# Attention and mixture-of-experts layer on one core: FFN steps spread over other slots, VectorE's exponential in two halves, loop branches announced

## What is computed

```python
def wl_step(acc, wl):
    cpm, iw = wl
    ...
    scores = jnp.einsum('bhqd,bhkd->bhqk', Qw, Kw) * SCALE
    scores = scores * jnp.cos(KERR * scores * scores)
    attn = jax.nn.softmax(scores, axis=-1)
    out = jnp.einsum('bhqk,bhkd->bhqd', attn, V)
    return (acc + out * iw, None)
...
logits = x @ router_w + router_b
probs = jax.nn.softmax(logits, axis=-1)
top_v, top_i = jax.lax.top_k(probs, TOP_K)
...
h = jax.nn.gelu(jnp.einsum('btd,edf->ebtf', x, w1), approximate=False)
y = jnp.einsum('ebtf,efd->ebtd', h, w2)
out = jnp.einsum('bte,ebtd->btd', gates[..., :E], y) + gates[..., E:] * x
...
x = _layernorm(x + _L0_attn_ref(x, ...), axis=-1)
x = _layernorm(x + _L0_ffn_ref(x, ...), axis=-1)
```

## Time and profile before

| | |
|---|---|
| median of 3 runs | 7504.47 us (7492.89 to 7508.42) |
| the profiled execution's own time | 7501.78 us |
| its span | 7500.2 us, 125933 instructions |
| ACT busy | 6970.5 us (93%) |
| PE busy | 6103.0 us (81%) |
| DVE busy | 5752.1 us (77%) |
| granted clock, mean | 0.93 |
| ACT line 556 (the exponentials) | 2048 instructions, 6765.2 us busy, mean 3392 ns, 318.5 us idle before them |
| PE line 626 (the weighings) | 30720 matmuls, 4092.8 us busy, mean 644 ns |

### The profile page before, as it was taken

How to read it: one execution, slowest core, us unless ns; L and a number is a source line. 1 busy time by engine, 2 the same in 40 slices (tenths; PEclk the granted TensorE clock), 3 DMA queues, 4 the chain that set the end, 5 groups by cost and what they waited for, 6 DMA issues and landing times.

```text
span 7500.2 us, 125933 instructions
## 1 busy us (share of the span) xinstructions
PE 6103.0 (81%) x46020; PEld 2156.8 (29%) x46020; DVE 5752.1 (77%) x7952; ACT 6970.5 (93%) x2227; POOL 117.5 (2%) x243
## 2 busy tenths in 40 slices
PE   6888887787888878888888888888888887888877
PEld 2222222222223322323232223222232332332325
DVE  4777777777787787778777787878787777877873
ACT  4999999999999999999999999999999999999992
POOL 0000000000000000000000000000000000000000
PEclk7999999999999999999999999999999999999998
DMA  2000000000000000001000000000010000000000
GB/s 57 4 4 4 2 4 4 4 5 13 28 15 26 28 15 28 22 20 31 22 24 28 14 27 25 18 28 19 25 31 17 26 28 14 28 22 21 28 18 35
DMA packets 61179, 152.18 MB, mean 20 GB/s; under 512 B 10272, under 2 KB 28576, under 8 KB 60320
## 3 DMA queue, kind: packets, MB, share of 16 engines
q1 hardware_dynamic: 59808, 142.14, 6.7%
q0 software_dynamic: 768, 1.57, 0.1%
HBM read 132.66 MB, written 11.01 MB: 19 GB/s over the span
## 4 chain that ended last, share of the span: by engine, by line
ACT 38%; PE 21%; issue 21%; DVE 14%; ACTq 5%; DMA 0%; DVEq 0%; SPq 0%
ACT ring L556 37%; PE pv L626 13%; ACTq L551 3%; DVE scores L762 3%; DVE vprobs L780 2%; DVE vprobs L781 2%; PE pv L633 2%; PE sc L609 1%; PE sc L598 1%; PE tr L642 1%; DVE vbits L779 1%; DVE vpower L777 1%; DVE ring L778 1%; DVE vbits L776 1%; PE sc L1076 1%
## 5 line engine op out<-in xcount | busy, mean ns | idle before, releaser
L556 ACT ACTIVATE ring<-scores 128x4096 f32<-128x4096 f32 (+3 forms) x2048 | 6765.2, 3392 | 318.5 <-PE pv L626 262.7
L626 PE MATMUL pv<-ring,vh 128*32 128x512 f32 x30720 | 4092.8, 644 | 1099.0 <-ACT ring L556 1053.7
L626 PEld LDWEIGHTS pv<-ring,vh 128*32 128x32 f32 x30720 | 1018.9, 116 | 3826.8 <-issue 2297.7
L788 DVE COPY numer<-pv 128x512 f32<-128x512 f32 x512 | 353.1, 690 | 913.5 <-PE pv L633 906.3
L752 DVE TENSOR_REDUCE rowmax<-sc 128x1 f32<-128x1024 f32 x512 | 602.1, 1217 | 163.4 <-PE sc L590 163.4
L781 DVE SCALAR_TENSOR_TENSOR vprobs<-vprobs,vbits 128x1024 f32<-128x1024 f32 x512 | 627.2, 1225 | 17.6
L780 DVE SCALAR_TENSOR_TENSOR vprobs<-ring 128x1024 f32<-128x1024 f32 x512 | 627.3, 1225 | 17.5
L782 DVE SCALAR_TENSOR_TENSOR vprobs<-ring,vprobs 128x1024 f32<-128x1024 f32 x512 | 627.2, 1225 | 17.6
L762 DVE COPY scores<-sc 128x1024 f32<-128x1024 f32 (+1 forms) x512 | 601.7, 1216 | 31.3 <-PE sc L609 30.7
L633 PE MATMUL pv<-vprobs,vlast 128*32 128x512 f32 x2048 | 530.4, 593 | 12.3 <-DVE vprobs L782 10.3
L633 PE MATMUL pv<-vpower,vlast 128*32 128x512 f32 x2048 | 529.6, 592 | 0.0
(11 more groups left out here) (159 smaller groups left out, 2684.0 us busy)
## 6 DMA issues: line engine op xcount, KB each, us to landing
tile_w<-in_L_ffn_w SPq DMA_DIRECT2D x192, 512.0 KB, 3.9
qt<-q_scratch SPq DMA_DIRECT2D x256, 36.0 KB
kt_<-k_scratch SPq DMA_DIRECT2D x256, 36.0 KB
ring<-in_L_ffn_w SPq DMA_DIRECT2D x2, 2048.0 KB, 12.3
scores<-in_L_attn_x SPq DMA_DIRECT2D x4, 512.0 KB, 4.8
q_scratch<-qt SPq DMA_DIRECT2D x4, 512.0 KB, 3.8
k_scratch<-kt_ SPq DMA_DIRECT2D x4, 512.0 KB, 4.0
v_scratch<-vv SPq DMA_DIRECT2D x4, 512.0 KB, 3.4
```

The costliest lines, as they stand in the source:

```text
L556: nc.scalar.activation(ring[:, i % SLOTS, 0:cols], scores[:, bass.ds(n % 2, 1), half * CK:(half + 1) * CK, :].rearrange("p o k s -> p (o k ...
L626: last = nc.tensor.matmul(sums, vh[:, buf, half * CK + k, :], ring[:, 2 * half + w2, col:col + HALF], start=(half == 0 and k == 0), stop=( ...
```

## The change

- **FFN steps.** In the first head TensorE's four single steps lie at steps 5, 9, 11 and 13 (before 5, 6, 7 and ahead of 8), VectorE's pieces at steps 5, 10, 11 and 13 (`TILE_SLOTS`). The slices go from steps 11 to 14 to steps 12 to 15. In the second head the parts of the second matmul go from 11 to 14 to 10 to 13, the gates from step 6 to step 4, and `tile_finish` is split: four additions at step 12 (`add_experts`, as soon as two parts are there), four at 13, then the layer norm at 13.
- **Guards.** TensorE's transposes of the numerators wait for the tile copies that share their PSUM tile at quarters 2 and 3, and those at the end for the logits; the projection and the router wait for `tr_read`.
- **ScalarE** takes the logits' exponential directly ahead of the Gelu, behind the first quarter of the second head.
- **Exponential in halves.** `exponents` (four operations) runs at even steps, `polynomials` (three) at odd ones; before, all seven ran at odd steps. The last step of a head was that of the next head's first set; now steps 14 and 15 are.

```diff
@@ scalar_main
-                quads(n, 0, 3)
+                quads(n, 0, 4)
+                quads(n + 1, 0, 1)
                 act.wait_ge(tile_logits_made, i + 1)
                 nc.scalar.activation(t_ex, t_lg, ACT.Exp).then_inc(tile_exp, 1)
-                quads(n, 3, 4)
-                quads(n + 1, 0, 1)
                 act.wait_ge(tile_hidden_copied, 4 * (i + 1))
...
@@ head_products
-                    if quad == 2 and wi == 0 and part == 1 and tile_no is not None:
-                        tile_router(pe, tile_no)
...
-                        if quad == 2 and part == 1 and tile_no is not None:
-                            pe.wait_ge(tile_logits_made, tile_no + 1)
+                        if part == 1 and tile_no is not None and quad == 2:
+                            pe.wait_ge(tile_attT_made, tile_no + 1)
+                        if part == 1 and tile_no is not None and quad == 3:
+                            pe.wait_ge(tile_x1T_made, tile_no + 1)
                         transpose_numer(pe, n, quad - 1)
...
-                        if quad == 1 and wi:
-                            if wi == 1:
-                                tile_attention(pe, tile_no, n)
-                            elif wi == 2:
-                                tile_projection(pe, tile_no)
-                            else:
-                                tile_transpose(pe, tile_no)
-                        elif 11 <= at < 15:
-                            tile_slice(pe, tile_no, n + 1, at - 11)
-                    if tile_no is not None and part == 2 and 11 <= at < 15:
-                        tile_part_two(pe, tile_no, n + 1 if more else n, at - 11)
+                        if at == 5:
+                            tile_attention(pe, tile_no, n)
+                        elif at == 9:
+                            tile_projection(pe, tile_no, n)
+                        elif at == 11:
+                            tile_transpose(pe, tile_no)
+                        elif at == 13:
+                            tile_router(pe, tile_no, n)
+                        if at >= 12:
+                            tile_slice(pe, tile_no, n + 1, at - 12)
+                    if tile_no is not None and part == 2 and 10 <= at < 14:
+                        tile_part_two(pe, tile_no, n + 1 if more else n, at - 10)
+            if part == 1 and tile_no is not None:
+                pe.wait_ge(tile_logits_made, tile_no + 1)
             transpose_numer(pe, n, 3)
...
-            with pe.Fori(0, PAIRS - FIRST_PAIR - 1) as i:
+            with nc.Fori(0, PAIRS - FIRST_PAIR - 1, engines=TENSOR_ONLY, hint_back_edge=True) as i:
...
@@ exponentials becomes exponents (to the fourth operation) and
+        def polynomials(dve, m, pair):
+            base = VSTEPS * (8 * m + pair)
+            probs = vprobs[:, pair % 2, :]
+            dve.wait_ge(vexp_step, base + 4)
...
+        def add_experts(dve, i, half, then):
+
+            dve.wait_ge(tile_parts, 4 * i + 2 * half + 2 + START)
+            for e in range(half * NE // 2, (half + 1) * NE // 2):
...
@@ vector_head
-                    if at == 8 and part == 1:
-                        tile_part_one_vector(dve, i, 3, then)
...
-                    if quad == 1 and wi and part == 1:
-                        tile_part_one_vector(dve, i, wi - 1, then)
-                    if 11 <= at < 15 and part == 1:
-                        copy_hidden(dve, i, at - 11)
-                    if at == 14 and part == 2:
+                    if at in TILE_SLOTS and part == 1:
+                        tile_part_one_vector(dve, i, TILE_SLOTS.index(at), then)
+                    if at >= 12 and part == 1:
+                        copy_hidden(dve, i, at - 12)
+                    if at in (12, 13) and part == 2:
+                        add_experts(dve, i, at - 12, then)
+                    pair = at // 2 + 1
+                    if pair < 8:
+                        (exponents if at % 2 == 0 else polynomials)(dve, n, pair)
+                    elif more:
+                        (exponents if at % 2 == 0 else polynomials)(dve, n + 1, 0)
+                    if at == 4 and part == 2:
+                        tile_gates(dve, i, then)
+                    if at == 13 and part == 2:
                         tile_finish(dve, i, then)
-                    if at == 6 and part == 2:
-                        tile_gates(dve, i, then)
-                    if at % 2 == 1 and at < 15:
-                        exponentials(dve, n, at // 2 + 1)
-                    elif at == 15 and more:
-                        exponentials(dve, n + 1, 0)
...
+        TILE_SLOTS = (5, 10, 11, 13)
```

More of the change, by code:

```diff
@@ L739, in tensor_main @@
                 shifted_tile(pe, 0, k)
-            with pe.Fori(0, FIRST_PAIR) as i:
+            with nc.Fori(0, FIRST_PAIR, engines=TENSOR_ONLY, hint_back_edge=True) as i:
                 head_products(pe, 2 * i, part=1)
                 head_products(pe, 2 * i + 1, part=2)
-            with pe.Fori(0, PAIRS - FIRST_PAIR - 1) as i:
+            with nc.Fori(0, PAIRS - FIRST_PAIR - 1, engines=TENSOR_ONLY, hint_back_edge=True) as i:
                 n = 2 * (i + FIRST_PAIR)
@@ L762, in copy_scores, with exponents @@
             nc.vector.tensor_copy(scores[:, bass.ds(m % 2, 1), k, :].rearrange("p o s -> p (o s)"), sc[:, use % 2, :]).then_inc(sc_free, 1)
-        def exponentials(dve, m, pair, first=False):
+        def exponents(dve, m, pair, first=False):
             base = VSTEPS * (8 * m + pair)
             score = scores[:, bass.ds(m % 2, 1), KT - 1, :].rearrange("p o s -> p (o s)")
-            bits, mant, power, probs = vbits[:, :], vmant, vpower[:, pair % 2, :], vprobs[:, pair % 2, :]
+            bits, power = vbits[:, :], vpower[:, pair % 2, :]
             then = stepper(dve, vexp_step, base, [0])
@@ L838, in tile_gates @@
             then(nc.vector.scalar_tensor_tensor(tile_z[:, :], tile_x1[:, :], t_route[6][:, 0, NE:NE + 1], tile_x1[:, :], ALU.mult, ALU.add))
-        def tile_finish(dve, i, then):
-            dve.wait_ge(tile_parts, 4 * (i + 1) + START)
-            for e in range(NE - 1):
-                then(nc.vector.scalar_tensor_tensor(tile_z[:, :], sc[:, 1, e * P:(e + 1) * P], t_route[6][:, 0, e:e + 1],
-                                                    tile_z[:, :], ALU.mult, ALU.add))
-            e = NE - 1
-            nc.vector.scalar_tensor_tensor(tile_z[:, :], sc[:, 1, e * P:(e + 1) * P], t_route[6][:, 0, e:e + 1],
-                                           tile_z[:, :], ALU.mult, ALU.add).then_inc(tile_added, 1)
+        def add_experts(dve, i, half, then):
+            dve.wait_ge(tile_parts, 4 * i + 2 * half + 2 + START)
+            for e in range(half * NE // 2, (half + 1) * NE // 2):
+                ins = nc.vector.scalar_tensor_tensor(tile_z[:, :], sc[:, 1, e * P:(e + 1) * P], t_route[6][:, 0, e:e + 1],
+                                                     tile_z[:, :], ALU.mult, ALU.add)
+                if e < NE - 1:
+                    then(ins)
+                else:
+                    ins.then_inc(tile_added, 1)
+        def tile_finish(dve, i, then):
             dve.wait_ge(tile_added, i + 1 + START)
@@ L897, in vector_main @@
                 copy_scores(dve, 0, k)
-            exponentials(dve, 0, 0, first=True)
-            with dve.Fori(0, H) as n:
+            exponents(dve, 0, 0, first=True)
+            polynomials(dve, 0, 0)
+            with nc.Fori(0, H, engines=VECTOR_ONLY, hint_back_edge=True) as n:
                 vector_head(dve, n)
@@ L908, in pair @@
                 assert counted[0] == TILE_STEPS, counted
-            with dve.Fori(0, PAIRS - FIRST_PAIR - 1) as i:
+            with nc.Fori(0, PAIRS - FIRST_PAIR - 1, engines=VECTOR_ONLY, hint_back_edge=True) as i:
                 pair(i, False)
```

19 lines of the change are left out of this document (12 added, 7 removed).

## The result

| | before | after |
|---|---|---|
| median | 7498.68 us (7483.6 to 7508.42, 4 runs) | 7212.52 us (7211.55 to 7216.38, 4 runs) |
| profiled execution, its span | 7501.78, 7500.2 us | 7212.97, 7211.4 us |
| granted clock, mean | 0.930 | 0.942 |

The ratio is 0.9621, with a 95% interval of 0.9603 to 0.9639: the change takes 286 us off.

What follows compares the result with a forecast made beforehand. ScalarE's chain of exponentials was taken as the bound, with only its 284.8 us idle behind TensorE to win. From 7501.78 us, −88.5 + 5 − 24.6 − 155.6 + 11 − 12.1 = −264.8 gave 7237, as median 7240; range 7215 to 7316.

Steps and rivals of the forecast that it cites:

- Part 1: FFN steps two slots apart in the first head: −88.5 us, with +5 for lateness at steps 12 to 15.
- a and b: ScalarE's waits for TensorE in the first head of the 24 FFN pairs, 66.4 and 22.1 us, both to go.
- c: ScalarE's waits in the second head, 11.0 and 17.6 us, to go but for 4 us behind the Gelu.
- T+11.4: forecast end of the first head's layer norm, T being the end of weighing 9; x1 asked for at T+13.2.
- Rival 4: Part 1 fails: layer norm at step 10 starts late, two thirds of a and b remain; 7300 us, chance 0.06.
- Part 2: exponential in halves and gates from step 6 to 4, spreading VectorE's work so c goes: −24.6 us.
- rival 3: slower: numerator copy at step 15 of every head late behind half an exponential; about 7604 us, chance 0.03.
- Part 3: loops' closing branches announced: −155.6 us at TensorE's FFN jump back, +11 left over, −12.1 in the loop without FFN.
- Rival 2: the announcement does nothing, waits at TensorE's jumps back stay, a to c go; 7397 us, chance 0.10.
- Rival 1: the second gap stays whole, 3 us a round, and steps 12 to 15 cost 1 us a pair; 7314, chance 0.12.
- the second gap: TensorE's 0.88 us break after six matmuls of the FFN loop body; 0 to 66 us might remain, 11 taken.
- The floor: least time if all ScalarE idle time at line 556 goes: −284.8 us, or 7220 on the median's scale.

Runs made afterwards that it cites:

- steps_only: the changed kernel with the whole exponential at odd steps and without the four announcements; 7375.09 us, ratio 0.9838.
- transpose_at_10: the changed kernel with TensorE's transpose of x1 one step earlier, at step 10 instead of 11; 7285.07 us, ratio 0.9708.
- hints_and_first_head: the kernel before with only TensorE's two loop announcements and the first head's moved FFN steps; 7231.58 us, ratio 0.9641.
- chains_broken: the changed kernel with ScalarE waiting four times a head, before an exponential, for the end of the one before; 7262.43 us, ratio 0.9683.
- no_hint_first_loop: the changed kernel with TensorE's loop over the pairs without FFN unannounced; 7221.52 us, ratio 0.9628.
- hints_only: the kernel before with the four loop announcements alone; 7335.17 us, ratio 0.9777.
- no_vector_hints: the changed kernel with VectorE's two loops unannounced; 7213.02 us, ratio 0.9611.

## Why the prediction came out as it did

**The bound.** Right. ScalarE's chain sets the pace and the rest is its idle time behind TensorE. Waits fell by 278.8 us, the span by 288.8.

**Part 1, the first head's steps (−88.5, +5).** Right: a and b are gone, and steps_only, without any announcement, is 123 us below before (part 1 and c together were worth 88.5 − 5 + 24.6 = 108 in the sum; the 14.4 us that it saves at the jump back were not in it). The layer norm that I had at T+11.4 and asked for at T+13.2 is there with more margin than those 1.8 us: it ends at 2545.63 by VectorE's timeline (below), and the transpose starts at 2549.25, 3.6 us later. Rival 4 did not happen. transpose_at_10 shows what one step less would have cost, 3.0 us a pair. The +5 for steps 12 to 15 was for nothing: no wait is left there.

```profile
2545.29 0.34 DVE L374 TENSOR_SCALAR tile_x<-tile_z,tile_small 128x128 f32<-128x128 f32 x1
```

**Part 2, halves and gates (−24.6).** The mechanism was right, the account was not. c is gone, and the residue I left in for slow weighings behind the Gelu, 4 us, measured 3.7 (6.0 less the entry's 2.33). But I credited two edits with one saving. Once the steps have moved and the jumps are announced, either of the two earns it (19 us, from hints_and_first_head), and the other is worth 0.4 to 1.7 us, within the spread of the runs. And the halves alone cost 60 us: rival 3's mechanism is real in the second heads with FFN work. That the layer norm's move to step 13 is what keeps it away I read from the order of the instructions; no run undoes that move alone.

**Part 3, the announcements (−155.6 + 11 − 12.1).** The mechanism was right. It is the largest part of the change: 155 us by taking it out of the change, 142 to 182 by putting it alone into the kernel before. Rival 2, that it does nothing, is out. The Trainium skill's sentence in Runtime: NRT & Kernel Launch (Instruction fetch mechanics), that prefetch is purely sequential, does not hold for an announced branch in these runs: the gap went from 3.35 to 0.17 us, and 49 packets fewer were fetched. Rival 1 is out too, and the +11 with it: the second gap does not stay, nor does any part of it. I had argued that code behind the head can be asked for only once the head runs. In place of that the rows show 32 matmuls without a break in all 22 rounds. Whether the announcement brings in the next block too, or the head merely no longer starts late, the runs do not tell apart. What the sum did not have is the price of leaving an announced loop, 2.33 us here.

**The floor.** This is the step that failed, and the reason why the time lies below the range. I set the floor at −284.8, or 7220: the idle time of ScalarE at line 556 and nothing else. That its exponentials' busy time would fall with the waits was put at nothing ("faster or slower move that by a few us"). It fell, from 6765.2 to 6752.4 us, 12.8, because each wait costs ScalarE the overlap of two exponentials besides its own length. chains_broken gives the price: 0.11 us of busy time per broken chain. There are 98 waits fewer, so some 10 us could have stood in the sum. The other 2.4 of the 12.8 are no gain. The logits' exponential stood between two exponentials, inside their overlaps, and now stands ahead of the table load, where its time shows. First before, then in the changed kernel:

```profile
2363.91 0.20 ACT L566 ACTIVATE tile_small<-tile_small 128x9 f32<-128x9 f32 x1
2364.01 52.81 ACT L556 ACTIVATE ring<-scores 128x4096 f32<-128x4096 f32 x16
```

```profile
2377.87 0.20 ACT L569 ACTIVATE tile_small<-tile_small 128x9 f32<-128x9 f32 x1
2378.09 1.28 ACT L571 ACT_TABLE_LOAD   x1
```

The stretch between the exponentials around a Gelu grew for it from 6.24 to 6.35 us, 2.5 us in 24 pairs. So waits and overlap give 278.8 + 12.8 − 2.5 = 289.1, and the span fell by 288.8. The mean of one exponential rose meanwhile, from 3392 to 3405 ns, and tells nothing of the speed: no_hint_first_loop has 3393 ns and nearly the same busy time (6753.2). The Trainium skill (ScalarE: Activation LUTs, What ACT_TABLE_LOAD costs) gives an overlap of about 93 ns for back-to-back ACTIVATEs; the trace agrees, with 0.11 us from the earlier trace rows and from chains_broken.

One run seems to speak against this price: hints_only has 48 waits fewer than before, and its exponentials are busy for 6766.2 us, no less. But 47 breaks of its chain are too short for the list of waits. Counted on the single instructions of the traces there are 107 breaks in it, nearly as many as the 117 of the kernel before; the changed kernel has 24.

**The sum, again.** Three sizes account for the 27 us. The residues that I left in were 5 + 4 + 11 = 20 us, and 6.0 were measured (3.7 behind the Gelu, 2.33 at the exit of the loop, which I had not thought of): 14. The overlap: 10. The scale: I put the median 2.7 us above the profiled execution's time, and the changed kernel's is 0.5 below it: 3. The residues alone could not have taken the time below 7220. The low end, 7215, stood 5 us below my floor, for which I had only "a few us"; with the overlap counted, the floor is near 7210, and the time lies 2.5 above it. I had read the one duration that tells of it (7.13 us for two exponentials) and not used it.

What stays open: why the waits in hints_only and transpose_at_10 differ from pair to pair, why the runs of hints_only fall in two groups, what makes the exit of one announced loop dearer than that of the other, and whether the place of the loop's head in its block plays a part in the second gap. No run moved it.

## What to carry to other kernels

Where an engine's loop body is too long to be held, look at its timeline at the jump back: a gap of some 3 us has slow matmuls behind it that cost 1.7 us and more, and here an announced branch took both away, for a gap of 4.04 us at the exit of one loop and of 0.42 at that of the other. When idle time goes from the engine that sets the pace, count the waits as well as their length: each also costs the overlap of two instructions, and together that was some 10 us of 289 here. And undo the parts of a change both from the whole and singly: two edits that cure the same wait each look worthless when taken from the whole, and one that is harmless in the whole cost 60 us alone.

## What the runs showed of the hardware that I had not expected

- With its branch announced, TensorE's loop over FFN pairs has no gap behind its head either, and moves two packets of instructions fewer per round (12 in place of 14 in one pair, 43 over 22 jumps), where the unannounced jump had two gaps.
- Leaving an announced loop cost 4.04 us of "issue" on TensorE in the one loop and 0.42 us in the other; the unannounced loops have none.
- VectorE's unannounced jump shows 1.25 us of "issue" (no_vector_hints), TensorE's 3.0 to 3.5 us (loop without FFN, before).
- After a pause of 7.90 us a weighing of TensorE takes 6.16 us in place of 3.64, after 4.04 us it takes 5.34, and after 6.39 us 25 of its matmuls take 5.50 in place of 3.19. The granted clock in these three stretches was 0.58, 0.68 and 0.57, and 1.00 in those of 3.64 and 3.19 us: after such a pause TensorE runs at 1.2 GHz for a while before it is back at 2.4. These pauses cost their length and 1.7 to 2.5 us more.
- Exponentials of 128x4096 in a row overlap by 0.11 us on ScalarE. A wait between them forfeits that and adds 0.09 us of idle time (0.21 in the loop without FFN), even when what it waits for is its own instruction before.
